# Grouping the transposes and value products of attention inside the second feed-forward layer (a fused cross-attention and gated MLP kernel, one core)

## The reference

```
x = x + xattn(layernorm(x), ctx)      # 8 heads of 32, causal mask, softmax over 77 keys
h = silu(x' w1) * (x' w2)             # x' = layernorm(x), hidden width 1024, ternary weights with scales
h = gelu(h h1); h = gelu(h h2)        # 1024 x 1024 each
x = x + h w3
```

## Time and profile before

| | |
|---|---|
| median of 3 runs | 1674.82 us (1674.29 to 1677.77) |
| the profiled execution, its time | 1673.74 us |
| its span (first to last instruction) | 1671.6 us |
| mean granted clock of PE | 0.985 of 2.4 GHz |
| PE busy | 1617.4 us, 97% |
| DVE busy, ACT busy | 806.5 us (48%), 783.5 us (47%) |
| a middle pass | 100.7 us (the same DVE instruction starts at 600.30 and at 701.00 us) |

### The profile page before, as it was taken

The page is one execution under the profiler, slowest core; times in us unless marked ns, Lnnn a source line. Parts: engine busy times, 40 slices in busy tenths (PEclk is TensorE's granted clock), DMA queues, the critical chain, the costliest instruction groups (busy, mean ns, idle before and its releaser), DMA issues.

```text
span 1671.6 us, 22062 instructions
## 1 busy us (share of the span) xinstructions
PE 1617.4 (97%) x9006; PEld 1311.9 (78%) x9006; DVE 806.5 (48%) x1255; ACT 783.5 (47%) x1126; POOL 139.4 (8%) x136
## 2 busy tenths in 40 slices
PE   5599999999999999999999999999999999999998
PEld 4378788787887878878787887878878787887887
DVE  5563634637255463634637255463544636345331
ACT  4463644636345363543636345363543635345342
POOL 1101102010010200102010010200102010010000
PEclk7699999999999999999999999999999999999999
DMA  8100000010000100000010000100001010000000
GB/s 328 43 1 26 29 25 29 0 42 13 25 29 0 54 0 25 29 25 29 0 42 13 25 29 0 52 2 25 29 11 43 0 40 14 25 30 1 1 13 13
DMA packets 17638, 48.40 MB, mean 29 GB/s; under 512 B 5584, under 2 KB 7760, under 8 KB 16208
## 3 DMA queue, kind: packets, MB, share of 16 engines
q1 hardware_dynamic: 17616, 48.09, 8.0%
HBM read 39.63 MB, written 8.45 MB: 29 GB/s over the span
## 4 chain that ended last, share of the span: by engine, by line
PE 88%; DVE 6%; ACT 3%; issue 2%; DMA 0%; POOL 0%; POOLq 0%; SPq 0%; ACTq 0%
PE ffn_banks L348 69%; PE att_banks L484 4%; PE att_banks L503 3%; PE att_banks L456 3%; PE att_banks L472 2%; PE att_banks L493 2%; PE att_banks L447 2%; DVE probs L702 1%; DVE total L698 1%; ACT L579 1%; ACT probs L579 1%; DVE a_f L662 1%; PE att_banks L442 1%; PE att_banks L511 1%; DVE a_lo L667 1%
## 5 line engine op out<-in xcount | busy, mean ns | idle before, releaser
L348 PE MATMUL ffn_banks<-a_hi,h_sb 128*128 128x512 f32 x1024 | 408.9, 399 | 0.0
L348 PE MATMUL ffn_banks<-b_hi,h_sb 128*128 128x512 f32 x1024 | 401.3, 392 | 0.0
L348 PE MATMUL ffn_banks<-a_lo,h_sb 128*128 128x512 f32 x1024 | 400.2, 391 | 0.0
L348 PE MATMUL ffn_banks<-b_lo,h_sb 128*128 128x512 f32 x1024 | 398.6, 389 | 0.0
L554 ACT ACTIVATE a_f<-ffn_banks,vec 128x512 f32<-128x512 f32 x128 | 88.2, 689 | 354.2 <-PE ffn_banks L348 354.2
L673 DVE TENSOR_TENSOR a_lo<-a_f,a_hi 128x512 fp32r<-128x512 f32 x128 | 88.6, 692 | 317.8 <-ACT a_hi L555 317.8
L348 PEld LDWEIGHTS ffn_banks<-a_hi,h_sb 128*128 128x128 f32 x1024 | 192.3, 188 | 48.9 <-issue 6.2
L348 PEld LDWEIGHTS ffn_banks<-b_lo,h_sb 128*128 128x128 f32 x1024 | 192.3, 188 | 39.8
L348 PEld LDWEIGHTS ffn_banks<-b_hi,h_sb 128*128 128x128 f32 x1024 | 192.3, 188 | 39.8
L348 PEld LDWEIGHTS ffn_banks<-a_lo,h_sb 128*128 128x128 f32 x1024 | 192.5, 188 | 38.5
L348 PE MATMUL ffn_banks<-ln_hi,w_sb 128*128 128x512 f32 x512 | 213.8, 418 | 6.2 <-issue 6.2
(11 more groups left out here) (89 smaller groups left out, 1952.5 us busy)
## 6 DMA issues: line engine op xcount, KB each, us to landing
x_in<-in_x SPq DMA_DIRECT2D x16, 512.0 KB, 3.5
h_bits<-in_h SPq DMA_DIRECT2D x8, 1024.0 KB, 20.8
out<-out_sb SPq DMA_DIRECT2D x16, 512.0 KB, 2.6
ln_t<-in_x_t SPq DMA_DIRECT2D x15, 512.0 KB, 4.3
ln_rows<-ln_rows_dram SPq DMA_DIRECT2D x15, 512.0 KB, 3.8
w_bits<-in_w SPq DMA_DIRECT2D x3, 1024.0 KB, 10.1
ctx_sb<-in_ctx_t SPq DMA_DIRECT2D x16, 154.0 KB, 3.6
w_att_sb<-in_w_att SPq DMA_DIRECT2D x1, 512.0 KB, 5.8
```

What stands on the lines that cost most here:

```text
L348: mm = nc.tensor.matmul(psum, left, right, start=(k == 0 and part == 0), stop=(k == rows - 1 and part == 1))
```

## The change

The steps are ordered anew in both lists. In `ORDER`, `PT` 0 stands behind `L2` 2 and directly before `PT` 1; `SOFT` 1 follows these two; `PT` 2 and `PT` 3 stand together behind `L2` 3; both value products stand together behind `L2` 4. The probabilities of batch 1 get a buffer of their own, `attn_t2`, which lies over `xln` and `out_sb` (those two become neighbours in SBUF); its first writers on ACT and DVE therefore wait until the last output tile is stored. `PT` 2 and `PT` 3 swap their bank pairs and wait for the copies of `PT` 0 and `PT` 1, and the wait of the value products is for all four blocks.

```diff
-    ("PT", 0), ("SOFT", 1), ("L2", 2), ("PT", 1), ("L2", 3), ("PV", 0), ("PT", 2), ("L2", 4), ("PT", 3),
-    ("L2", 5), ("PV", 1), ("L2", 6), ("L2", 7),
+    ("L2", 2), ("PT", 0), ("PT", 1), ("SOFT", 1), ("L2", 3), ("PT", 2), ("PT", 3),
+    ("L2", 4), ("PV", 0), ("PV", 1), ("L2", 5), ("L2", 6), ("L2", 7),
...
-    ("PT", 0), ("PT", 1), ("CHECK", 3), ("SOFT", 1), ("ROUND", 1), ("PV", 0), ("PT", 2), ("PT", 3), ("CHECK", 4),
+    ("PT", 0), ("PT", 1), ("CHECK", 3), ("SOFT", 1), ("ROUND", 1), ("PT", 2), ("PT", 3), ("PV", 0), ("CHECK", 4),
...
-        xln, _ = put("xln", [P, NQ, D])
+        xln, xln_at = put("xln", [P, NQ, D])
+        out_sb, out_at = put("out_sb", [P, NQ, D])
+        assert out_at == xln_at + 4 * NQ * D
+        attn_t2, _ = put("attn_t2", [TK, H, TQ], at=xln_at)
...
-                        if n == 3:
-                            pe.wait_ge(heads_done, NB * a + 1)
-                        pair = (2, 0, 0, 2)[n]
+                        if n >= 2:
+                            pe.wait_ge(pt_act_done, NQ * a + n - 1)
+                            pe.wait_ge(pt_dve_done, NQ * a + n - 1)
+                        pair = (2, 0, 2, 0)[n]
...
-                        pe.wait_ge(pt_act_done, NQ * a + 2 * n + 2)
-                        pe.wait_ge(pt_dve_done, NQ * a + 2 * n + 2)
+                        if n == 0:
+                            pe.wait_ge(pt_act_done, NQ * a + NQ)
+                            pe.wait_ge(pt_dve_done, NQ * a + NQ)
...
-                                                      attn_t[:, 4 * g + h, :], start=True, stop=True)
+                                                      (attn_t, attn_t2)[n][:, 4 * g + h, :], start=True, stop=True)
...
+                        if n == 2 and f is not None:
+                            dve.wait_ge(stored, 16 * f + 16)
+                        nc.vector.tensor_copy((attn_t, attn_t2)[n // 2][:, 4:8, q0:q0 + P],
+                                              ab[0:TK, (2, 0, 2, 0)[n] + 1, :].rearrange("p (h q) -> p h q", h=4))\
```

More of the change, by code:

```diff
@@ L138, in build_kernel @@
         x_in, _ = put("x_in", [P, NQ, D])
-        xln, _ = put("xln", [P, NQ, D])
+        xln, xln_at = put("xln", [P, NQ, D])
+        out_sb, out_at = put("out_sb", [P, NQ, D])
+        assert out_at == xln_at + 4 * NQ * D
+        attn_t2, _ = put("attn_t2", [TK, H, TQ], at=xln_at)
         ln1_t, _ = put("ln1_t", [P, KD, TILE])
         x1_keep, _ = put("x1_keep", [P, NQ, D])
-        out_sb, _ = put("out_sb", [P, NQ, D])
         k_t, _ = put("k_t", [P, HG, NB * TK])
@@ L583, in one_pass @@
                         q0 = (n % 2) * P
-                        pair = (2, 0, 0, 2)[n]
-                        nc.scalar.copy(attn_t[:, 0:4, q0:q0 + P],
+                        pair = (2, 0, 2, 0)[n]
+                        if n == 2 and f is not None:
+                            act.wait_ge(stored, 16 * f + 16)
+                        nc.scalar.copy((attn_t, attn_t2)[n // 2][:, 0:4, q0:q0 + P],
                                        ab[0:TK, pair, :].rearrange("p (h q) -> p h q", h=4)).then_inc(pt_act_done, 1)
@@ L705, in one_pass @@
                         q0 = (n % 2) * P
-                        nc.vector.tensor_copy(attn_t[:, 4:8, q0:q0 + P],
-                                              ab[0:TK, (2, 0, 0, 2)[n] + 1, :].rearrange("p (h q) -> p h q", h=4))\
+                        if n == 2 and f is not None:
+                            dve.wait_ge(stored, 16 * f + 16)
+                        nc.vector.tensor_copy((attn_t, attn_t2)[n // 2][:, 4:8, q0:q0 + P],
+                                              ab[0:TK, (2, 0, 2, 0)[n] + 1, :].rearrange("p (h q) -> p h q", h=4))\
                             .then_inc(pt_dve_done, 1)
```

## The result

The changed kernel takes 1754.35 us (median of 4 runs, 1752.03 to 1755.91); the kernel before, run beside it, 1674.55 us. The ratio is 1.0473, with a 95% interval of 1.0452 to 1.0493: 80 us slower. The forecast was 1751 us.

A forecast was written before the change was run, and what follows sets the result against it. PE, busy 97% of the span, was taken as the bound. Removed wait, merging, added wait and prologue gave 48.5 us; with 28 us for the clock, 76.5 us over 1673.74 us, forecast 1751 us, range 1716 to 1786 us.

The forecast's parts named there:

- the main term: PE's new wait at the third transposes (`PT` 2) for the delayed `SOFT` 1: 4.25 us a pass, 63.8 us.
- the term of the attention of tile 0: In the prologue, batch 0's value product now lies on the chain to the projection: 2.0 us more, bounds 1 to 3.
- The removed wait: PE's wait at the first transposes of each pass goes away: 0.87 us less in 15 passes, 13.0 us.
- The added wait: At the third transposes PE waits for `SOFT` 1, moved later on DVE: 4.25 us a pass, 63.8 us.
- The merging: Five visits to the attention banks become three in each pass: 0.3 us less a pass, 4.5 us in all.
- The clock: PE's clock falls during the new waits, slowing transposes and the following product: 28 us, half of the 56 us bound.
- the clock's half: Taking 28 of 56 us for the clock; called mis-sized if the clock stayed at 1.00 or fell in every pass.
- Half the passes at the full price: One reading of the 28 us: the clock falls in half of the passes, costing 3.7 us each time.
- The first rival: Dense work around the new wait keeps PE's clock up in the passes: 1723 us, chance 0.20.
- the second as a size: Rival: the clock falls in every pass at the full price, 3.7 us each, 56 us: 1779 us, chance 0.20.
- The prologue: Attention of tile 0: batch 0's value product delays the projection by 2.0 us, one product at that stretch's clock.
- The faster rival: `SOFT` 1 on DVE is in time, so the passes get no new wait: 1659 us, chance 0.06.

The follow-up runs named there:

- experiment 5: Kernel before, attention visits one `L2` step later on PE and ACT, DVE doing first copy and `SOFT` 1 before `L2` 2's subtraction, nothing merged: 1662.91 us, 0.9920.
- Experiment 1: Changed kernel with only `SOFT` 1 moved one place up, ahead of `L2` 2 on DVE: 1672.03 us, 0.9981 of the kernel before.
- experiment 2: Changed kernel with DVE's own order (copy of `PT` 0, `SOFT` 1, copy of `PT` 1, subtraction of `L2` 2): 1655.53 us, 0.9885 of the kernel before.
- experiment 3: Changed kernel with 18 identity matmuls on PE filling the wait before the third transposes in each pass: 1721.17 us, 1.0270 of the kernel before.
- experiments 6 and 7: Changed kernel with 9 and with 5 identity matmuls before the third transposes: 1735.24 us (1.0349) and 1737.95 us (1.0365) against the kernel before.

## Why the prediction was right

The mechanism of the main term was right, and so was its size. The size of the clock term was right by luck, and the term of the attention of tile 0 isn't confirmed.

**The removed wait** (13.0 us) came out as said: experiment 5 measures 13.4 us for it.

**The added wait** (4.25 us a pass, 63.8 us) is 4.26 us in the pass read and 64.1 us over the trace. Each link is in the trace: `L2` 2 directly behind `L2` 1, the table load directly behind the exponential, DVE idle between the two subtractions, both copies, then `SOFT` 1. Experiment 1 shows that the place of `SOFT` 1 in DVE's program is the cause: one step up, and the wait of 4.26 us is 0.9 us. The reading that made the sum right was to follow three programs at once; DVE's busy time is the same before and after, and the list of waits names the same pair and the same count of 17.

**The merging** (0.3 us a pass, 4.5 us) is 0.4 to 0.45 us, 6 to 7 us. Counted as the prediction counted them, by the pieces of the chain, the five visits of experiment 5 take 5.64 us and the three of experiment 2 take 5.36 us: 0.28 us, as was taken. The term was undersized since only the visits themselves were counted. The rest, some 0.16 us, lies in the feed-forward products beside them, in part in the slower start of the product behind each visit.

**The clock** (28 us) is 32.1 us by the trace and 33 us by experiment 3. The choice of half the bound was a guess between 0 and 56 us, and that it landed near is luck: the clock fell in all 15 passes, which the prediction itself had named as a sign that the clock's half was mis-sized. Half the passes at the full price, the first of its two readings, is out. The second, all passes with one of the two parts, comes near, but both parts were paid: of the 32.1 us, 21.1 lie in the transposes and 11.0 in the product behind. The transposes paid in full in 11 passes, 1.66 us more; the 1.97 us taken for them had set a row that runs from the start of the first to the modelled end of the last (3.71 us) against two pieces of 0.87 us that run from end to end. The product behind paid 0.6 us in the pass shown instead of 1.74, because the low stretch began in the wait, where it costs nothing, and ended early in the product. The first rival, the clock stays up, is out, and so is the second as a size: every pass falls, but at 2.1 us each, not 3.7. The Trainium skill, "TensorE: Matmul & The Clock Gate", section "HAM oscillation — how this bites in real kernels", had the pattern right, a fall at every wait; the full price that was tied to its rule did not come.

**The prologue** (2.0 us): in the trace of the changed kernel the first feed-forward matmul is 1.96 us later, but the experiments don't bring that back when the order is undone: it starts at 75.92 and 76.31 with the old order, and at 76.38, 74.73 and 75.51 with the new one. The term isn't confirmed, and the 1.96 us may be chance.

**The faster rival** said that `SOFT` 1 in time would give 1659 us. Experiment 2 made it so and gave 1655.5 us.

## What to carry to other kernels

Where one list orders all engines, moving a step for the sake of one engine also moves it on the others. Here PE's transposes were well placed one product later, while the same move put 4.4 us of DVE's work and waiting ahead of an instruction that PE needs next. Write out each engine's own program around the step, mark which instruction is the next to be waited for, and let nothing stand ahead of it that nobody waits for; an order of its own for one engine costs a few lines. A new wait of a few microseconds on TensorE should be priced with a clock term on top, here half of the wait again.

## What the runs showed of the hardware

- The clock fell in all 15 passes with waits of 4.1 to 4.3 us, in 10 of 15 with 3.0 or 2.2 us left idle behind identity matmuls (experiments 6 and 7), and in none with 0.9 us (experiment 1). Where it falls differs from pass to pass: 2 us after the last matmul in the pass shown, and only after the transposes had begun in four others (sixteen transposes of 3.20, 2.67, 2.52 and 2.50 us in place of 3.67). Shortening the idle time from 3.0 to 2.2 us changed nothing in what the clock cost (16.8 and 16.7 us); filling it did away with the cost, and the time was 14 us shorter than with 2.2 us left.
- Matmuls of the identity by itself, 18 of 128 columns in float32, 4.2 us, kept the clock up through the wait.
- A visit to other banks with float32 matmuls costs little beyond its own work: some 0.1 us ahead of it if it begins with value products and nothing if it begins with transposes, and some 0.1 us behind it, where the second matmul of the following product starts 0.31 to 0.34 us after the first instead of 0.23. Five visits merged into three gave 0.4 to 0.45 us a pass.
